# A four-layer cross-attention model on one core: the order of every engine's steps planned with finer offsets

## The reference

```python
x = x + L0_xattn(layernorm(x), ctx)      # 16 heads of 16, softmax
x = x + L0_ffn(layernorm(x))             # ternary weights, relu squared, hidden 1024
x = x + L1_xattn(layernorm(x), ctx)
x = x + L1_ffn(layernorm(x))             # product keys: 4 heads x 8 rows of a table
x = x + L2_xattn(layernorm(x), ctx)      # with rotary positions
x = x + L2_ffn(layernorm(x))             # 8 experts (top 2) and 2 shared ones
x = x + L3_xattn(layernorm(x), ctx)      # autocorrelation
x = x + L3_ffn(layernorm(x))             # 8 experts, top 2, with a bias
```

## Time and profile before

| | |
|---|---|
| runs, us | 1690.18, 1690.42, 1696.91 (median 1690.42) |
| span of the profiled execution, us | 1689.5 |
| PE, DVE, ACT, POOL busy, us | 1316.3, 1113.8, 816.4, 690.3 |
| mean granted TensorE clock | 0.865 |
| first and last gather start, us | 318.2, 1161.8 |

### The profile page before, as it was taken

One profiled execution on the slowest core, in us unless ns is written; L12 is line 12 of the kernel. 1 busy time (PEld: TensorE's weight loads), 2 busy tenths in 40 slices (PEclk: granted clock), 3 DMA queues, 4 the chain that ended last, 5 costly groups with the idle time before them and its releaser, 6 DMA issues.

```text
span 1689.5 us, 18810 instructions
## 1 busy us (share of the span) xinstructions
PE 1316.3 (78%) x5858; PEld 660.2 (39%) x5858; DVE 1113.8 (66%) x2929; ACT 816.4 (48%) x2055; POOL 690.3 (41%) x705
## 2 busy tenths in 40 slices
PE   5789886756788687586576778768979977886998
PEld 2345443332254334333224433433533533532444
DVE  5542417689986867998989898787732451436355
ACT  2345442757657677565674577567426220310110
POOL 2000000388888888828888688875000100000000
PEclk8789997977889797779587689789989988898999
DMA  5000000376556767717656666654010211021000
GB/s 221 22 1 1 10 5 3 81 180 183 151 158 164 197 155 218 185 36 187 173 165 217 175 176 182 166 153 127 7 16 1 82 39 31 1 51 45 1 13 25
DMA packets 59381, 169.07 MB, mean 100 GB/s; under 512 B 15632, under 2 KB 20304, under 8 KB 58640
## 3 DMA queue, kind: packets, MB, share of 16 engines
q0 software_dynamic: 40960, 134.25, 29.6%
q1 hardware_dynamic: 18320, 33.61, 6.2%
HBM read 163.00 MB, written 4.82 MB: 99 GB/s over the span
## 4 chain that ended last, share of the span: by engine, by line
PE 34%; POOL 31%; issue 12%; DVE 12%; DMA 6%; ACT 4%; SPq 1%; POOLq 0%; DVEq 0%; ACTq 0%
POOL bufR L1841 26%; PE psum L1174 6%; POOL half_sum L1855 4%; PE psum L1040 3%; PE psum L1118 2%; DVE bufB L1531 2%; DMA bufR<-in_table,rowid 2%; PE psum L1097 2%; PE psum L844 2%; PE psum L1052 2%; PE psum L975 2%; PE psum L967 1%; PE psum L811 1%; PE psum L896 1%; PE psum L893 1%
## 5 line engine op out<-in xcount | busy, mean ns | idle before, releaser
L1841 POOL DMA_INDIRECT bufR<-in_table,rowid x512 | 549.1, 1072 | 247.2 <-issue 124.5
L1199 ACT ACTIVATE bufR<-bufR 128x256 f32<-128x256 f32 x512 | 205.6, 405 | 79.8 <-DVE bufR L1404 79.4
L1404 DVE TENSOR_TENSOR bufR<-bufR 128x1024 f32<-128x1024 f32 x128 | 163.1, 1275 | 63.7 <-DMA bufR<-in_table,rowid 63.5
L1040 PE MATMUL psum<-xtf,wf 128*128 128x512 f32 x320 | 158.5, 641 | 29.3 <-DVE x_sb L1467 13.3
L844 PE MATMUL psum<-bufB 32*128 32x308 f32 x768 | 99.8, 597 | 102.5 <-DVE bufB L1531 80.2
L1531 DVE TENSOR_REDUCE bufB<-psum 128x8 f32<-128x1232 f32 x96 | 137.8, 1436 | 50.5 <-PE psum L844 50.2
L1868 POOL TENSOR_TENSOR x_sb<-x_sb,wattn 128x256 f32<-128x256 f32 x16 | 11.0, 728 | 295.4 <-DMA wattn<-in_attn 165.0
L1052 PE MATMUL psum<-wf,bufR 128*128 128x256 f32 x320 | 91.1, 437 | 35.7 <-DVE bufR L1679 33.4
L1208 ACT ACTIVATE bufR<-bufR,ew 128x256 f32<-128x256 f32 x128 | 64.1, 503 | 113.0 <-DVE ew L1412 113.0
L1861 POOL TENSOR_TENSOR x_sb<-x_sb,wattn 128x256 f32<-128x256 f32 x32 | 25.4, 823 | 227.9 <-DMA wattn<-in_attn 169.9
L1467 DVE TENSOR_TENSOR x_sb<-x_sb,psum 128x256 f32<-128x256 f32 x128 | 50.1, 415 | 97.9 <-PE psum L975 62.9
(11 more groups left out here) (236 smaller groups left out, 2534.8 us busy)
## 6 DMA issues: line engine op xcount, KB each, us to landing
bufR<-in_table,rowid POOLq DMA_INDIRECT x512, 4.3
wf<-in_ffn SPq DMA_DIRECT2D x2, 2304.0 KB, 15.3
bufR<-in_ffn SPq DMA_DIRECT2D x1, 2696.5 KB, 17.2
wattn<-in_attn SPq DMA_DIRECT2D x4, 641.0 KB, 6.0
wf<-in_rope SPq DMA_DIRECT2D x4, 512.0 KB, 6.2
bufB<-in_ffn SPq DMA_DIRECT2D x1, 2048.0 KB, 8.4
scr_corr<-bufR SPq DMA_DIRECT2D x16, 128.0 KB, 2.4
bufR<-scr_corr SPq DMA_DIRECT2D x4, 512.0 KB
```

Source lines behind the costliest of these rows:

```text
L1040: ins = mm(bank(6 + r), gu[:, kt, r, :], xtf[:, kt, :], start=kt == 0, stop=kt == KT - 1)
L1199: own.mark(act(row, row, ACT.Identity, accum_out=dots[:, g % 4, j:j + 1]))
L1404: tt(rows, rows, cast(xg[c % 2][:, i, :].unsqueeze(1), [P, GRP, D]), ALU.mult).then_inc(f1_mu, 1)
L1841: eng.indirect_dma_start(ring[:, s * GRP + j, :], None, io["table"], bass.IndirectOffsetOnAxis(ap=rowid[c % 2][:, at + j:at + j + 1], axis ...
```

## The change

The offsets of `PREFER` are replaced, and an offset can now be given for the first n parts of a step's name, for any kind: ("o", 0, 2) is the step o of layer 0 in chunk 2. A step gets the sum of all that fit it. Before, an offset was for a kind, or for a kind and layer for ten kinds. Kinds, durations, waits, banks and instructions are as they were; only the five lists can differ.

```diff
--- before.py
+++ after.py
@@ -87,14 +87,14 @@
 
 
 PREFER = dict(
-    PE={('Q', 1): 20, ('X', 'f'): 20, ('X', 'z'): 5, ('be3',): 40, ('mt', 0): -20, ('o', 0): -20, ('o3',): 5, ('s', 2): 30,
-        ('t', 0): 45, ('u3',): -10, ('w', 0): 5, ('y2',): 5, ('y3',): 10},
-    ACT={('N4',): 10, ('Q', 1): 10, ('X', 'q'): 20, ('lg2',): -50, ('mt', 0): 10, ('q3',): 5, ('sc',): 70, ('tk1',): -40,
-        ('w', 1): 5, ('w', 2): 40},
-    DVE={('ad',): 5, ('l3',): 20, ('lg2',): -5, ('low',): -5, ('p1', 1): 90, ('p1', 2): 25, ('sm1',): -5, ('t', 1): 30,
-        ('t', 2): -5, ('tern',): 10, ('y', 0): -10, ('y', 1): 10, ('y3',): 5},
-    POOL={('ad',): 5, ('bo3',): 20})
-BY_LAYER = ('p1', 'mt', 's', 'r', 'w', 't', 'o', 'y', 'X', 'Q')
+    PE={("be3",): 130, ("co", 0): 50, ("h0",): -65, ("o", 0, 2): 100, ("o", 2, 2): 25, ("o3", 0): -20, ("o3", 0, 1): 100, ("tp",
+        0): -40, ("u3",): -10, ("y", 2, 2): -25, ("y2", 2): -20, ("y3",): 630},
+    ACT={("N4", "a"): 40, ("gu1", 2): -5, ("gu1", 3, 0): -20, ("lg2",): -85, ("q1",): -20, ("r", 0): -10, ("s", 2, 0): 80,
+        ("sc",): 75, ("tk1",): -105},
+    DVE={("N3",): 10, ("ad",): 5, ("gu2", 0): -5, ("ix1", 1): -5, ("kv",): -275, ("lg2",): -10, ("p1", 1): 365, ("p1", 2): 25,
+        ("p1", 2, 2): 40, ("sm1",): -5, ("sm1", 3, 2): -90, ("t", 0): -10, ("tern", 0): 145, ("tern", 2, 0): -325},
+    POOL={("ad",): 185},
+)
 
 
 Z_BANKS = (2, 4)
@@ -447,8 +447,8 @@
     for n in reversed(list(todo)):
         rank[n] = todo[n][0] + todo[n][2] + max([lag + rank[m] for m, lag in after[n]], default=0.0)
     for (engine, item) in todo:
-        kind = item[:2] if item[0] in BY_LAYER else item[:1]
-        rank[engine, item] += PREFER.get(engine, {}).get(kind, 0.0)
+        offsets = PREFER.get(engine, {})
+        rank[engine, item] += sum(offsets.get(item[:n], 0.0) for n in range(1, len(item) + 1))
     free, begin, waiting = {}, {n: 0.0 for n in todo}, {n: len(first) for n, (_, first, _) in todo.items()}
     order = {e: [] for e in ("PE", "ACT", "DVE", "POOL", "SP")}
     ready = {e: [n for n in todo if n[0] == e and not waiting[n]] for e in order}
```

## The result

| | kernel before | changed kernel |
|---|---|---|
| runs beside each other, us | 1690.18 to 1699.21 (median 1693.66, 4 runs) | 1664.53 to 1675.26 (median 1670.87, 4 runs) |
| span of the profiled execution, us | 1689.5 | 1673.5 |
| mean granted TensorE clock | 0.865 | 0.87 |

The ratio is 0.9869, with a 95% interval of 0.984 to 0.9899: 1.3% faster. The profiled pair differs by 16.0 us and the medians by 22.8. The profiled execution of the changed kernel was its slowest (1675.26 us), so the traces show some 16 us of the gain, and what follows speaks of these.

What follows compares the result with a forecast made beforehand. No engine bounds the whole: POOL waits until 318.2 us, its gathers set a floor to 1175.3, then PE sets the pace. -1.5 - 4.0 - 8.6 = -14.1 us on 1689.5 gave 1676 us; eight-in-ten range 1655 to 1701.

Steps and rivals of the forecast that it cites:

- Saturated offsets: Large offsets on several engines (layer 1 maxima, y3, be3, half sums, ternary weights, h0) move nothing that counts: 0 us.
- the 5 us given: First stage, before the first gather: worst case of a loss of some 5 us from steps that pass a maximum.
- Row numbers: Chunk 2's row numbers on DVE: kv put behind them, so POOL's next gather starts earlier; -1.5 us, between -4.1 and +1.1.
- the 5 us that I named as a sign: Chunk 2's first gather, at 755.2, moves by less than 5 us against the one before it.
- the upper bound of +1.1: Worst case at chunk 2's row numbers: DVE waits for ACT's exponential and starts them 1.1 us later.
- First hole: PE's 9.7 us wait before tp in the first correlation: chunk 2's last steps cross co and fill part; -4.0 us.
- Second hole: PE's 8.6 us wait before o3 in the first correlation: last chunk's gate and output steps fill it; -8.6 us.
- A sign that I had named for being wrong: DVE, held in order behind a late transfer, stops PE at a place where it does not now.
- The 10.4 us hole: PE in the last stage, behind a DVE waiting for layer 3's values: stays, as its step has no offset.
- the second correlation's: PE's two holes of 4.7 and 4.6 us at the second correlation: both stay.
- That rival, with the filler lost: Second correlation's holes grow as expert steps are spent earlier, +9.0 us, 1699 us; chance 0.18 with another in-order stall.
- the early row numbers: Rival: chunk 2's attention comes forward and wins 15.5 us of POOL's holes, 1660 us; chance 0.14 (below 1665).

Runs made afterwards that it cites:

- e2: Kernel before with all of the change's offsets except PE's of the last stage, which stay as before; ratio to the kernel before 1.0012 [0.9982, 1.0042].
- e3: Kernel before with one offset more, tp of the first batch at -40; ratio to the kernel before 0.9929 [0.99, 0.9957], median 1700.8 us.
- e1_tail: Kernel before with the change's PE offsets of the last stage, without before's small one for the last transposes; ratio to the kernel before 0.9973 [0.9935, 1.001].
- f1: The changed kernel itself, repeated on the same chip as f2; 1671.57 us, ratio to the kernel before 0.9866 [0.9838, 0.9893].
- f2: The changed kernel with the offset of tp of the first batch back at 0; 1676.76 us, ratio to the kernel before 0.9893 [0.9869, 0.9918].
- g1: The changed kernel with only the planner's times of the values' exchange as measured (32 reads issued over 15.1 us, not 1.6); ratio to before 0.9866.

## Why the prediction was right, and where not

**Saturated offsets, 0.** Right as far as tried. e2 has all of them on the other engines, and h0, and gains nothing; the first gather is 2.5 us later, inside the 5 us given. y3 and be3 on PE were not tried apart; the stretch behind the second correlation is the same (196.4 and 196.5).

**Row numbers, -1.5 us.** The size was in the noise, and the step failed: kv was not put behind them. Chunk 2's first gather came 6.2 us later, and 3.5 us later counted from the last gather before it: within the 5 us that I named as a sign, but above the upper bound of +1.1. It cost nothing at 1175 us: POOL's waits for a place in the ring fell from 10.7 to 4.4 us. The rule of the Trainium skill ("SBUF — State Buffer", section "Who interferes with whom") on VectorE's scaling steps met no test, since these steps still run where no gather does.

**First hole, -4.0 us.** The mechanism was wrong. I had chunk 2's last steps cross the correlation, and held that nothing else could be PE's work there. They stayed ahead of it; a gate step and the queries of the last chunk went ahead of tp, and the hole fell by 9.0 us, to 0.7. I had passed over the two steps directly behind tp as candidates.

**Second hole, -8.6 us.** Right in place and size: the hole is 0, with gate and output steps of the last chunk in it. That o3's offset is needed for it was only half right: e3 closes 6.4 us of it by tp alone.

**What the sum lacked.** The clock behind a hole: -2.8 us at tp and -2.8 at o3. Against it stand new waits: 4.2 us for DVE ahead of two gate steps in place of 1.1, and one of these slow (5.40 us): the filler that went forward came at the pace of DVE, which builds the rolls (L1733, L1735) between its parts of these steps. -9.0 - 8.6 - 5.6 + 3.1 + 1.7 = -18.4 us, where 16.9 were measured; the rest is spread over small waits. That the whole came within 2 us of the traces (14.1 forecast, 16.0) is in part luck. The first hole gave 5.0 us more than I took and the clock 5.6 us that the sum left out; the new waits and the slow gate step took 4.8 us back, small waits more, and the 1.5 us at the row numbers did not come. A sign that I had named for being wrong, DVE stopping PE where it did not before, did come, with 3.1 us and not behind a transfer.

**What stays.** The 10.4 us hole and the second correlation's (5.0 and 3.1 us, before 4.7 and 4.6) stayed, as forecast. That rival, with the filler lost, did not come; nor did the early row numbers. The forecast of 1676 us is 5 us above the median, since 2 us more were won in the traces and the rest lies between profiled runs and medians.

**What stays open.** Why the stretch of the gathers takes 15 to 40 us more on some chips. In e1_tail POOL's sums waited 37.8 us behind ACT's scaling, 16.1 in the kernel before; whether late landings or late sums begin it was not tried. Open too is what o3's offset does alone, and which offset outside the last stage keeps chunk 2's last steps ahead of the correlation in the changed kernel, where e1 lets them cross.

## What to carry to other kernels

In a planned order, compare the planner's assumed time of each transfer with the trace before tuning ranks: here right times with coarse offsets did at least as well as fine offsets with wrong times. Look at every engine that stands in order before a late transfer, and ask which finished input of another engine waits behind it: one step of 2.9 us on VectorE, standing too early, cost 12 us on TensorE. Judge a part of such a change by undoing it in the full one as well as by doing it alone (5 us and 14 us here), since a planner's answer to one offset depends on the others.

## What the runs showed of the hardware

A hole of TensorE costs more than itself. Behind holes of 6.3 to 10.4 us, in before, after, e1, f1, f2 and g1, the next step took 5.4 to 6.5 us and not 3.6, at a granted clock of 0.56 to 0.66, and o3's half behind 8.6 us took 11.6 and not 8.8. Behind the new waits of 0.7 us and none the clock was 1.00. A short wait is not always safe: the gate step behind 2.8 us took 5.40 us at 0.69, and one behind 1.25 and 0.35 us took 3.70 us in the changed kernel's first trace and 5.40 in f1, in the same order. 32 reads of 10 KB each kept SP's queue for 15.1 us, 0.47 us apiece, though the median one landed in 1.7 us.
